# Linear-attention decoder layer: key products with an operand in PSUM, key sums after the updates' transposes, and multiplications of ones at a slot's end

## The reference

```python
def _L0_attn_ref(x, ln_g, ln_b, w_qkvb, b_qkvb, w_out, b_out):     # B=8, T=512, NH=16, D=16
    normed = (x - mu) * lax.rsqrt(var + LN_EPS) * ln_g + ln_b
    q, k, v, beta_pre = jnp.split(normed @ w_qkvb + b_qkvb, 4, axis=-1)
    beta = jax.nn.sigmoid(beta_pre)
    k = k / jnp.maximum(jnp.linalg.norm(k, axis=-1, keepdims=True), NORM_EPS)
    def step(S, inp):                                               # S: (b, NH, D, D)
        q_t, k_t, v_t, beta_t = inp
        retrieval = jnp.einsum('bhij,bhj->bhi', S, k_t)
        S = S + jnp.einsum('bhi,bhj->bhij', beta_t * (v_t - retrieval), k_t)
        o_t = jnp.einsum('bhij,bhj->bhi', S, q_t)
        return (S, o_t)
    _, out_t = lax.scan(step, S0, (q, k, v, beta))
    return x + out_t.transpose(1, 0, 2, 3).reshape(b, t, NH * D) @ w_out + b_out
```

## Time and profile before

| | us |
|---|---|
| median of 3 runs (lowest to highest) | 1035.82 (1035.44 to 1038.0) |
| the profiled execution, its own time | 1035.35 |
| its span, first to last instruction | 1033.5 |
| busy PE, DVE, ACT, POOL | 880.8, 867.2, 659.6, 545.7 |
| scan loop, from the first to the last solve's end | 39.5 to 673.7 |

### The profile page before, as it was taken

The page is one execution under the profiler, slowest core; times in us unless marked ns, Lnnn a source line. Parts: engine busy times, 40 slices in busy tenths (PEclk is TensorE's granted clock), DMA queues, the critical chain, the costliest instruction groups (busy, mean ns, idle before and its releaser), DMA issues.

```text
span 1033.5 us, 19418 instructions
## 1 busy us (share of the span) xinstructions
PE 880.8 (85%) x6218; PEld 674.9 (65%) x6225; DVE 867.2 (84%) x2448; ACT 659.6 (64%) x1663; POOL 545.7 (53%) x499
## 2 busy tenths in 40 slices
PE   7798999999989999999899899888999922995275
PEld 7586777777777777877777677655666621542164
DVE  4689899999999989889998879856677787899887
ACT  4677677776667756757666566345677651894095
POOL 6355476476456646644664554355678870880000
PEclk9899999999999989989998899999999975998599
DMA  9800000000000000002100000140420000000012
GB/s 163 138 3 10 6 6 11 7 7 10 8 7 8 10 6 6 8 9 80 55 11 7 6 6 10 29 125 21 155 79 1 1 1 1 1 1 1 1 67 97
DMA packets 28572, 30.49 MB, mean 30 GB/s; under 512 B 5548, under 2 KB 23864, under 8 KB 28472
## 3 DMA queue, kind: packets, MB, share of 16 engines
q1 hardware_dynamic: 28256, 29.12, 11.3%
q10 hardware_dynamic: 216, 0.14, 0.0%
HBM read 20.85 MB, written 4.19 MB: 24 GB/s over the span
## 4 chain that ended last, share of the span: by engine, by line
DVE 43%; PE 40%; issue 9%; ACT 4%; POOL 3%; DVEq 0%; ACTq 0%; POOLq 0%
PE ps L1862 6%; DVE arena L1283 5%; DVE arena L1291 5%; PE ps L2048 4%; DVE arena L1344 3%; PE ps L1932 3%; DVE arena L1269 3%; DVE arena L1272 3%; PE psY L1900 3%; PE psX L2069 3%; PE psY L2069 2%; PE ps L2247 2%; DVE arena L1336 2%; PE psG L2048 2%; DVE arena L1264 2%
## 5 line engine op out<-in xcount | busy, mean ns | idle before, releaser
L509 POOL TENSOR_SCALAR_AFFINE_SELECT arena<-arena 128x2048 f32<-128x2048 f32 x32 | 64.4, 2013 | 269.2 <-DVE arena L1272 262.7
L524 POOL TENSOR_TENSOR work<-work,half 128x16 f32<-128x16 f32 x32 | 93.8, 2931 | 2.7
L1924 PE MATMUL ps<-work 32*128 32x256 f32 x512 | 84.6, 406 | 10.2 <-ACT arena L713 10.1
L513 POOL TENSOR_SCALAR_AFFINE_SELECT arena<-arena 128x2048 f32<-128x2048 f32 x32 | 92.1, 2877 | 2.2
L678 ACT ACTIVATE arena<-ps,nparity 32x256 f32<-32x256 f32 x124 | 51.1, 457 | 63.8 <-PE ps L1862 63.4
L1924 PEld LDWEIGHTS ps<-work 32*128 32x128 f32 x512 | 54.7, 186 | 45.4 <-issue 27.1
L713 ACT ACTIVATE arena<-ps 128x512 f32<-128x512 f32 x128 | 68.9, 589 | 14.1 <-PE ps L1924 13.7
L1862 PE MATMUL ps<-work,arena 128*128 128x64 f32 x496 | 61.4, 277 | 19.3 <-DVE work L1308 19.2
L1862 PEld LDWEIGHTS ps<-work,arena 128*128 128x128 f32 x496 | 58.7, 193 | 28.8 <-issue 28.6
L1900 PE MATMUL psY<-work,arena 128*128 128x96 f32 (+1 forms) x512 | 69.1, 301 | 5.6 <-DVE arena L1362 5.6
L1900 PEld LDWEIGHTS psY<-work,arena 128*128 128x128 f32 x512 | 67.5, 216 | 6.4 <-DVE arena L1362 6.4
(11 more groups left out here) (344 smaller groups left out, 2548.7 us busy)
## 6 DMA issues: line engine op xcount, KB each, us to landing
arena<-in_mask_BxSxS_ik SPq DMA_DIRECT2D x8, 1024.0 KB, 6.8
xs<-arena SPq DMA_DIRECT2D x256, 16.0 KB, 1.8
arena<-in_ctx SPq DMA_DIRECT2D x8, 512.0 KB, 4.3
out<-xs SPq DMA_DIRECT2D x32, 128.0 KB, 1.7
arena<-in_x SPq DMA_DIRECT2D x8, 288.0 KB, 18.0
arena<-in_L_ffn_w SPq DMA_DIRECT2D x2, 1024.0 KB, 22.0
arena<-in_x SPq DMA_DIRECT2D x16, 96.0 KB, 6.4
arena<-in_L_attn_w_qkvb SPq DMA_DIRECT2D x2, 512.0 KB, 5.0
```

What stands on the lines that cost most here:

```text
L509: G.affine_select(out=keys, in_=keys, compare_op=ALU.is_ge, fill=0.0, base=0, pattern=[[0, NH], [1, P]], channel_multiplier=-1).then_inc(h ...
L513: G.affine_select(out=pairs, in_=pairs, compare_op=ALU.is_ge, fill=0.0, base=0, pattern=[[0, NH], [-CT, B], [0, CT]], channel_multiplier=1 ...
L524: own(G.tensor_tensor(root, length, half, ALU.pow))
L1924: last = M.matmul(ps[(2, 0)[r % 2]][:, f * 2 * P:(f + 1) * 2 * P], kq[j % 4][rows, f * P:(f + 1) * P], qe[rows, f].rearrange("p e t -> p ( ...
```

## The change

On DVE, keys_normed(j + 2) moves to directly behind keys_turned; scale_near is split, and its last two instructions (scale_pairs) come behind the state's copy; far_products works one chunk further ahead, on j + 2, with two buffers PF in turn; far_products and near_products take one operand from a copy of the key in ps[1] for all but the first two chunks; fold_near comes last before start_chunk. ACT makes that copy (key_copied_out) as the first thing of a slot. On PE and ACT the key sums move behind the updates' transposes, with a wait of PE for the near products, and PE multiplies ones twice at a slot's end, after a wait for ACT's betas. ACT's input moments are split: the sums stay ahead of the attention copies, except in slot 0, and the squares go between queries and betas. POOL's factors (FACTORS_AT) come one slot earlier, two cross-attention queries leave slot 27 for slot 28, and the ternary weights' sums go from ps[1] to psG, ahead of near_gram.

```diff
@@ -51,7 +51,7 @@
 X_GROUPS = [(0, 2), (2, 8), (8, 14), (14, NCK)]
 MOMENT_SLOTS = 8
 STAT_GROUPS = [(0, 2), (2, 8), (8, 14), (14, 20), (20, 26), (26, NCK)]
-FACTORS_AT = {2: 2, 4: 3, 6: 4, 8: 5}
+FACTORS_AT = {1: 2, 3: 3, 5: 4, 7: 5}
 ORDER = [(0, 0), (0, 1), (0, 2), (1, 0), (1, 1), (1, 2), (0, 3), (1, 3)] + [(b, w) for b in range(2, B) for w in range(NW)]
@@ -60,7 +60,7 @@
 EARLY = [n for n in range(NT) if ORDER[n][1] < 2]
 LATE = [n for n in range(NT) if ORDER[n][1] >= 2]
-QUERIES_AT = {20: 2, 21: 2, 22: 2, 23: 2, 27: 1, 28: 1, 29: 2, 30: 4}
+QUERIES_AT = {20: 2, 21: 2, 22: 2, 23: 2, 28: 2, 29: 2, 30: 4}
 ROW_NORMS_AT = {18: 0, 26: 1, 30: 2}
 GROUPS = [(4 * q, 4 * q + 4) for q in range(7)] + [(28, 30), (30, 32)]
@@ -210,7 +210,7 @@
         third = at[0]
         G2, G3, G4 = take(512), take(512), take(128)
         prod = take(1024)
-        take(1024)
+        PF = [PR[:, 0:1024], take(1024)]
         red = take(128)
         assert at[0] - third >= NW * (D + S)
         sexp_flat, kexp_flat, wq_flat = take(NH * P), take(NH // 2 * P), take(DC * 4 * D)
@@ -366,7 +366,7 @@
              "hq_ready hq_T hqT_ready up_mm act_own gabs "
              "gr_ready gc_ready ga_ready gd_ready down_mm out_ready stored").split()]
         yn_ready, hr_ready, hs_ready, tok_mm, picked, cand_ready = [sem(n) for n in "yn_ready hr_ready hs_ready tok_mm picked cand_ready".split()]
-        mixed_out = sem("mixed_out")
+        mixed_out, key_copied = sem("mixed_out"), sem("key_copied")
         last_known, q_early, att_moments, hid_moments, last_moments, xbeta_late = [
             sem(n) for n in "last_known q_early att_moments hid_moments last_moments xbeta_late".split()]
         (means_known, squares_known, q_known, yn_known, hn_known, hn_ready, xbeta_ready, y_scaled, x2_ready, h_scaled,
@@ -729,6 +729,11 @@
                 act.wait_ge(rn_ready, m)
                 A.activation(nrm[0], ps[1][:, 0:NH], ACT.Copy, scale=-1.0).then_inc(seeded, 1)
+            def key_copied_out(m):
+
+                act.wait_ge(k_ready, m + 1)
+                A.activation(ps[1][:, CW:2 * CW], kq[m % 4][:, 0:CW], ACT.Copy).then_inc(key_copied, 1)
+
             def mixed_copied(j):
                 act.wait_ge(w_mm, j + 1)
@@ -787,7 +792,7 @@
             x_moments = Chain(act, x_sums)
-            def input_moments(k):
+            def input_sums(k):
                 first = 8 + 3 * k
@@ -799,6 +804,10 @@
                     done = x_moments.issue(A.activation(scrap[i % 2], xc[:, i, :], ACT.Copy, accum_out=mean[:, i:i + 1]))
                 x_moments.need(done)
                 x_moments(A.activation(mean[:, first:first + 3], mean[:, first:first + 3], ACT.Copy, scale=-1.0 / D))
+
+            def input_squares(k):
+
+                first = 8 + 3 * k
                 for i in range(first, first + 3):
                     x_moments.need(x_moments.k - 1)
                     x_moments.issue(A.activation(scrap[i % 2], xc[:, i, :], ACT.Square, bias=mean[:, i:i + 1],
@@ -827,9 +836,9 @@
             def early_work(j):
-                if j < MOMENT_SLOTS:
-                    input_moments(j)
-                elif j < MOMENT_SLOTS + 2:
+                if 1 <= j < MOMENT_SLOTS:
+                    input_sums(j)
+                elif MOMENT_SLOTS <= j < MOMENT_SLOTS + 2:
                     for p in range(4 * (j - MOMENT_SLOTS), 4 * (j - MOMENT_SLOTS) + 4):
                         weights_summed(p)
                 elif 12 <= j < 16:
@@ -1005,12 +1014,12 @@
             early_tiles = iter(range(2 * B))
             for j in range(NCK + 1):
                 m = j + 3
+                if j >= 1 and exists(j + 1):
+                    key_copied_out(j + 1)
                 if j >= 1 and exists(j):
                     state(j)
                 if exists(j - 1):
                     updates_out(j - 1)
-                if j >= 1 and exists(j + 2):
-                    key_sums_out(j + 2)
                 if exists(j):
                     queries_by_parity(j)
                 if j >= 1 and exists(j + 3):
@@ -1019,6 +1028,8 @@
                     keys_spread(j)
                 if exists(j - 1):
                     updates_turned(j - 1)
+                if j >= 1 and exists(j + 2):
+                    key_sums_out(j + 2)
                 if j == NCK:
                     query_turned(2)
                     context_whole(1, 0)
@@ -1041,6 +1052,10 @@
                     outputs_turned(j - 1)
                 if exists(m):
                     queries(m)
+                    if j == 0:
+                        input_sums(0)
+                    if j < MOMENT_SLOTS:
+                        input_squares(j)
                     betas(m)
                     keys(m)
                 if m == NCK:
@@ -1239,8 +1254,7 @@
             def ternary_factors():
                 v.wait_ge(abs_sum, 1)
-                v.wait_ge(seeded, 15)
-                own(V.tensor_reduce(wsum[:, :], ps[1][:, 32:40].rearrange("p (k n) -> p k n", k=2), AX.X, ALU.add))
+                own(V.tensor_reduce(wsum[:, :], psG[:, 896:904].rearrange("p (k n) -> p k n", k=2), AX.X, ALU.add))
                 own(V.tensor_scalar(gam[:, :], wsum[:, :], 1.0 / (FF * D), 1e-5, ALU.mult, ALU.add))
                 V.reciprocal(rgam[:, :], gam[:, :]).then_inc(factors_ready, 1)
@@ -1298,7 +1312,7 @@
             def keys_normed(m):
                 v.wait_ge(rn_T, m + 1)
                 if m >= 2:
-                    v.wait_ge(seeded, min(m + 2, NCK))
+                    v.wait_ge(kraw_ready, min(m + 2, NCK))
                 key = kq[m % 4][:, 0:CW]
                 V.tensor_tensor(key, key, turned_norms_bank(m), ALU.mult).then_inc(k_ready, 1)
@@ -1323,6 +1337,10 @@
                                 over_s(bt.rearrange("p (q t) -> p q t", t=8)[:, :, 4:8], 4), ALU.mult)
                 V.tensor_tensor(g3[:, :, :, 0:2], psG[:, 512:768].rearrange("p (q t s) -> p q t s", t=2, s=2),
                                 over_s(bt.rearrange("p (q t) -> p q t", t=4)[:, :, 2:4], 2), ALU.mult)
+
+            def scale_pairs(m):
+
+                bt = beta[m % 4]
                 own.issue(V.tensor_tensor(G4, psG[:, 768:896], bt.rearrange("p (q t) -> p q t", t=2)[:, :, 1], ALU.mult))
                 odd = "p (q a) -> p q a"
                 V.tensor_tensor(g3[:, :, 1, 2], psG[:, 768:896].rearrange(odd, a=2)[:, :, 1],
@@ -1337,22 +1355,31 @@
                                     G4.rearrange("p (q a b) -> p q a b", a=2, b=1)[:, :, 1].broadcast_to([P, NH * 4, 2]), ALU.mult))
                 own.issue(V.tensor_tensor(g3[:, :, 1, 0:2], g3[:, :, 1, 0:2], folded, ALU.add))
+            def later_keys(m, t):
+
+                bank = kq[m % 4][:, 0:CW] if m < 2 else ps[1][:, CW:2 * CW]
+                return bank.rearrange("p (q t) -> p q t", t=t)
+
             def far_products(m):
                 v.wait_ge(k_ready, m + 1)
-                v.wait_ge(g1_mm, 2 * m)
+                if m >= 2:
+                    v.wait_ge(g1_mm, 2 * (m - 1))
+                    v.wait_ge(key_copied, m - 1)
                 key = kq[m % 4][:, 0:CW].rearrange("p (q t) -> p q t", t=16)
-                V.tensor_tensor(PR[:, 0:1024].rearrange("p (q t s) -> p q t s", t=8, s=8),
-                                over_s(key[:, :, 8:16], 8), over_t(key[:, :, 0:8], 8), ALU.mult).then_inc(prod1, 1)
+                V.tensor_tensor(PF[m % 2].rearrange("p (q t s) -> p q t s", t=8, s=8),
+                                over_s(later_keys(m, 16)[:, :, 8:16], 8), over_t(key[:, :, 0:8], 8), ALU.mult).then_inc(prod1, 1)
             def near_products(m):
                 v.wait_ge(g2_mm, m)
                 v.wait_ge(k_ready, m + 1)
+                if m >= 2:
+                    v.wait_ge(key_copied, m - 1)
                 for n, first in ((4, 1024), (2, 1536)):
                     key = kq[m % 4][:, 0:CW].rearrange("p (q t) -> p q t", t=2 * n)
                     V.tensor_tensor(PR[:, first:first + 16 * 8 * n].rearrange("p (q t s) -> p q t s", t=n, s=n),
-                                    over_s(key[:, :, n:2 * n], n), over_t(key[:, :, 0:n], n), ALU.mult)
+                                    over_s(later_keys(m, 2 * n)[:, :, n:2 * n], n), over_t(key[:, :, 0:n], n), ALU.mult)
                 key = kq[m % 4][:, 0:CW].rearrange("p (q t) -> p q t", t=2)
-                V.tensor_tensor(PR[:, 1792:1920], key[:, :, 1], key[:, :, 0], ALU.mult).then_inc(prod2, 1)
+                V.tensor_tensor(PR[:, 1792:1920], later_keys(m, 2)[:, :, 1], key[:, :, 0], ALU.mult).then_inc(prod2, 1)
             def state(j):
                 v.wait_ge(s_mm, j)
@@ -1489,11 +1516,12 @@
             far_products(0)
             keys_turned(0)
             scale_near(0)
+            scale_pairs(0)
             fold_near(0)
             start_chunk(0)
             for j in range(NCK + 1):
                 if j == 0:
-                    solve(0, {4: ((keys_normed, 1),), 8: ((near_products, 1),)})
```

(34 more changed lines are left out.)

## The result

The changed kernel takes 1006.34 us (median of 4 runs, 1001.88 to 1009.1), against 1036.91 us (1035.44 to 1038.14) for the kernel before on the same chip: a ratio of 0.9696, 95% interval 0.9664 to 0.9729. The profiled execution took 1005.02 us for a span of 1003.1 us, 30.4 us less span than before. The forecast was 1007, so its sum is right, but two of its terms are too small and one is too large.

The account below looks back on a forecast made before the run. DVE bounds the kernel before, TensorE the changed one. Gains of 10.7 (plain slots), 13.1 (long slots) and 5 (start) sum to 28.8 us: 1035.8 - 28.8 = 1007 us, range 998 to 1023.

Parts of the forecast that it names:

- DVE loses 1.73 us to POOL, and the change takes this away: Three DVE instructions per slot lengthened beside POOL's, 0.80 + 0.41 + 0.52 us; PSUM operands and a later fold avoid it.
- DVE and retrieval loop of 18.66 us: Slot length if DVE and the retrieval bound the changed kernel: 8.15 + 10.51 us.
- TensorE loop of 18.44 + 0.40 + 0.50 = 19.34: Slot length with TensorE as bound: 18.44 us, plus 0.40 for moved key sums and 0.50 for two ones.
- The slots' term: Plain slots fall from 19.71 to 19.34 us: 0.37 x 29 = 10.7 us gained.
- The long slots, 13.1 us: Of 15.9 us that longer slots add, all but one low-clock stretch of 2.75 us goes.
- The start, 5 us: Before the slots, TensorE's 4.09 us wait for ACT goes and part of the low clock may; gain -1 to 7.
- ACT's key copy at nothing: ACT's new key copy fits in 1.1 us before the state's copy; cost taken as 0, bounds 0 and 0.4.
- Rival A: TensorE is lengthened less, ones or key sums falling into a wait; slot 18.7 to 18.9, 993 us; 8%.
- Rival B: More low-clock stretches, four to ten in 29 slots, as the wait before the retrieval grows; six give 1021 us; 16%.
- Rival C: Key norms on POOL become the bound, margin 0.2 us; each slot loses 0.2 to 0.4, 1013 to 1018 us; 8%.
- Rival D: DVE products with a PSUM operand wait for POOL as well; DVE keeps 19.7 us a slot, 1018 us; 4%.
- Rival E: Key norms on POOL hold off the solve's two-SBUF products; solve grows by up to 4.2 us, about 1105 us; 3%.

Follow-up runs that it names:

- experiment 6: Changed kernel with far and near products reading both operands from SBUF again, order, waits and ACT's copy kept; 1005.5 us, ratio 0.97.
- experiment 8: Changed kernel without ones at the slot's end, key sums back ahead of the retrieval, six ones in the start's retrieval wait; 989.98 us, ratio 0.9559.
- experiment 4: Kernel before the change with only the two multiplications of ones added at the slot's end; 1027.71 us, ratio 0.9932.
- experiment 5: Kernel before the change with the ones and the rearranged side work (factors, queries, ACT's input moments); 1020.55 us, ratio 0.9834.
- experiment 9: Changed kernel without ones at the slots' ends, eight ones in TensorE's wait before the loop's first retrieval; 989.74 us, measured again 988.85 us.
- experiment 3: Changed kernel with the two ones moved from the slot's end into TensorE's wait ahead of the retrieval; 990.08 us, ratio 0.9581.

## Why the prediction came out right, step by step

- **DVE loses 1.73 us to POOL, and the change takes this away.** Right. The fold is at 0.29 us twice and the far product at 1.23, and experiment 6 brings 1.0 us of the loss back by the operands' place alone. DVE ends products and fold at +7.83 instead of the +7.47 forecast: the state's copy starts at +3.17, not +2.59, because TensorE, now the bound, begins the state at +1.23 instead of +0.59, and 0.44 of that is the ones.
- **DVE and retrieval loop of 18.66 us.** Right: slots 29 and 30 of the changed kernel, in which TensorE has neither key sums nor ones, are 18.66, and experiment 8 reaches 18.80 with 0.14 us explained by L1297.
- **TensorE loop of 18.44 + 0.40 + 0.50 = 19.34.** Measured 19.26. Without the ones it is 18.81, where 18.84 stood in the sum, so 18.44 and the key sums are right together; the ones are 0.45 and not 0.50, half of four of them up to the next group in the earlier trace rows, which came behind a wait. The slots' term is 29 x 0.45 = 13.1 us and not 10.7.
- **The long slots, 13.1 us.** 15.7 were gained (28.75 - 13.05). I left one low stretch of 2.75 us; there is none. The causes of the low stretches are as told: experiment 4 removes five by shortening the 1.13 us wait, experiment 5 the last two by the side work. A third cause was overlooked, 1.9 of the 15.9 us: slots 11 to 15 take 20.0 to 20.4 us at full clock. Experiment 5 still has them; in its slots 12 to 15 one of the solve's products stands beside POOL's L539 and takes 0.47 instead of 0.18 us, while slot 11 is the one with the ternary weights' factors. In the changed kernel slots 12 to 15 take 19.26 and slot 11 19.48. One reading was loose: six slots, not seven, take 21.4 us or more in the kernel before; the seventh low stretch lies in a slot of 20.11 us.
- **The start, 5 us.** Got 1.4: the mis-sized term. TensorE's wait shrank from 4.09 to 1.05 us as told, and so far it is right. But I had counted part of the low clock as given back, and the clock is low at the first retrieval: 6.89 us (5.38 before, 3.79 at 2.4 GHz in experiment 9). TensorE waits 2.01 us ahead of it for DVE's state copy (1.22 before), as key normalisation stands ahead of that and waits for ACT's keys, but the longer wait doesn't decide it: in experiment 5 the retrieval takes 6.91 us behind a wait of 1.22, in experiment 6 it takes 3.79 behind 2.02. Both profiles of the changed kernel have the stretch; in two without it (experiment 6, and the kernel without ones in 9) slot 1 starts at 62.1 instead of 66.1, a gain of 5.4.
- **ACT's key copy at nothing.** Right: it takes 0.39 us, ends at +2.21, and the state's copy begins at +3.17. (That no row shows a copy of 256 columns at over half of 1.1 us was loose: the L926 of the earlier trace rows takes 0.60 for as many.)
- **Rival A** (additions hidden) is false for this kernel and true in experiment 3. **Rival B** (more low stretches): the wait before the retrieval is 0.68 us, against 0.8 forecast, and the clock doesn't fall. **Rival C** (key norms late): the margin is 1.0 us, not 0.2. ACT's copy of the key sums comes at +9.29, POOL's last instruction ends at +13.38, TensorE turns them at +14.36. From copy to end it is 4.09 us and not the 4.62 that the earlier trace rows gave. L523 takes 0.25 us instead of 0.87, as it now stands beside products of 16 elements only and no longer beside the far product, which had two SBUF operands:

```profile
365.12 0.25 POOL L523 TENSOR_SCALAR work<-work 128x16 f32<-128x16 f32 x1 [3.19 <-ACT work L730]
365.46 3.02 POOL L524 TENSOR_TENSOR work<-work,half 128x16 f32<-128x16 f32 x1
368.54 0.40 POOL L526 COPY work<-work 128x256 f32<-128x256 f32 x1
```

- **Rival D** (PSUM products held too) is false by the same slot: L1369 takes 1.23 us beside L572's undisturbed 0.73, and start to start they overlap whole. **Rival E** (key norms in the solve hold its products) is false for L524, which is long, and true for the short L526 and L539: experiment 8 shows them at 0.14 and 0.30 us. (Its price was also added up wrong: 3.5 us in 29 slots on top of 1007 is 1109 us, not 1105.)

That the sum is right to 1 us is luck in part: +2.4 on the plain slots and +2.6 on the long ones against -3.6 on the start.

## What to carry to other kernels

Work that keeps TensorE busy is free only in a wait of TensorE; once the engine beside it has become faster, the wait is gone, the clock holds by itself, and the same instructions are on the path (+9.3 us in the kernel before, -12.4 in the changed one). So test each such filling again after the change that it comes with, and put it into the longest wait that is left. And the loop that an edit frees sets the price of what it adds: write down both loops of a slot, as 18.66 and 19.34 here, and the difference is what the additions cost and what a further edit can win.

## What the runs showed of the hardware

- **Whoever starts first keeps the way to SBUF.** DVE's two-SBUF product lengthened POOL's add from 0.73 to 1.73 us when it began 0.07 us earlier (experiment 6), and POOL's masks lengthened DVE's products when they began first. The Trainium skill's page "SBUF — State Buffer", section "SBUF: two separate sides", says so: the pair of ports is an exclusive lock of the instruction that starts first. These traces agree.
- **Not every POOL instruction holds DVE off.** L524 takes 3.0 us and lies over products with two SBUF operands that keep their 0.29 us, while L526, 0.40 us, lengthens one by 0.14 us and L539 one by 0.30 (experiment 8). The same section's wording, that the lock holds for the whole instruction, doesn't fit L524; it is a power over only 16 elements a partition, L526 a copy of 256.
- **A product with an operand in PSUM costs DVE no more than one without**: 1.23 us against 1.22 for 1024 elements, 1.02 against 1.03 for the two near ones (the kernel before, slot at 492.10, where POOL doesn't hold them).
- **The clock in the start differs from execution to execution** of one kernel with the same waits: a retrieval of 3.79 or 6.82 us, 3 to 4 us of the whole time. In slots 1 to 29 of the same kernel, where no wait of TensorE is longer than 0.9 us, it never fell. The Trainium skill's page "TensorE: Matmul & The Clock Gate", in "Part 1: The HAM clock gate", says that the window in which the chip watches TensorE is free-running, so that how many of a kernel's first multiplications run at the low clock varies from run to run. The two retrievals come 48 us into the kernel and fit that, which doesn't show that it is the cause.
